# Loading the three bf16 terms of the layer-3 queries one by one, each after its own store

## The chip, the cores and the metric

The kernel runs on one core of one Trainium2 chip. The metric is the device time of one execution in microseconds (us); lower is better.

## The reference

Eight batches go through four cross-attention layers in a row. The change lies in the last one, layer 3. Cut to what matters, it computes for every batch (c = 128 channels, 16 heads of d = 8, 256 query and 256 key positions):

```
q = einsum('oc,bct->bot', Wq, x) + bq      # x: what layer 2 returned
k = einsum('oc,bct->bot', Wk, kv) + bk     # kv: the context
v = einsum('oc,bct->bot', Wv, kv) + bv
attn = softmax(einsum('bhqd,bhdk->bhqk', q * d ** -0.5, k))     # d = 8
mean = einsum('bhqk,bhkd->bhqd', attn, v)
ex2  = einsum('bhqk,bhkd->bhqd', attn, v * v)
std  = sqrt(relu(ex2 - mean * mean))
out  = (instance_norm(x) * std + mean) * mask
```

## The kernel before

The batches b = 0 to 7 follow each other, and within a batch the layers 1, 2 and 3; layer 0 of batch b + 1 is laid between them. Each engine has its program written out in order: SP issues the transfers (DMAs), PE the matmuls, ACT, DVE and POOL the rest, and semaphores join them. An engine whose next instruction waits does nothing else, so on SP every later transfer waits too.

**The terms.** A head of layer 3 has only 8 channels. To get fp32-like products from bf16 matmuls, queries and keys are each cut into three bf16 terms: `h` (the value rounded to bf16), `m` (what is left, rounded) and `l` (what is left of that). They are made in the tile `parts` (128 channels x 3 terms x 256 positions), whose rows are heads times channels. The matmul wants another layout: in `Qx` and `Kx` (partitions x 16 heads x 256 positions) the channels and terms of a head stand below each other on partitions 0 to 71, so that one product over 100 partitions sums all nine pairs of terms. Rows 72 to 99 hold the mask and the shift by the row maximum.

**The way of the terms.** One store per term goes from `parts` to a scratch tensor in DRAM, `q_parts` or `k_parts` (3 terms x 8 channels x 4096 values), and three loads bring 24 rows each back. Each load has 24 rows of 8 KB, 192 KB in all. For the nine pairs, one side repeats a term three times in a row (24 rows of one term) and the other lists the three terms (8 rows of each) three times. Before the change, `Kx` has the repeated order and `Qx` the listed one:

```
for j in range(3):      # in key_terms, L596
    sp.dma_start(Kx[24 * j:24 * j + 24], k_parts[j:j + 1].to_broadcast([3, 8, NH * D]))\
for j in range(3):      # in query_terms, L604
    sp.dma_start(Qx[24 * j:24 * j + 24], q_parts).then_inc(ld_qx, 16)
```

**Who makes the query terms.** ACT rounds `h` from the projection of `q3` (`highs3`, L1329). DVE takes the rest (L1747) and makes `m` and `l` (L1757, L1759) between other work, a few us later. ACT and POOL do the same for the keys earlier in the batch (L1501, L1973, L1975). SP stores a term when its semaphore stands (`store_terms`, L587).

**Who waits for them.** PE's `scores3(b, 0)` waits for all of `Kx` and `Qx` (`ld_kx`, `ld_qx`) before its first product, L883 in the profile. Before it PE has layer 0's scores of the next batch and the maxima of layer 3 (L700, L725, L731); these take their own bf16 copies of queries and keys, not `Qx`. After it come seven more such groups of `scores3`, between other units in an order written out in `BOTH` (`LAST3` for the last batch, which has no layer 0 beside it; there `idle_products`, L909, fill PE's time with products that nobody reads).

**What SP does around it.** In a batch: the layer-2 weights, the stores and loads of the key terms, the stores and loads of the query terms, the weights of layer 1 (`load_mlp`, `WA` and `WB`, 1024 KB each, L529 and L530), the inputs of the next batch (`load_inputs`, `load_z`), and the regrouping of layer 3's sums through `scratch`.

Of the kernel before, what the change touches and what calls it, by code (L numbers as in the profile page):

```python
# [30 lines left out]
D = 256  # L31
NH = 16
# [150 lines left out]
def build(nc, z_in, ctxT_in, ctx_in, mask1, mask2, mask3, w0, wo, w1qk, w1v, w1o, w1a, w1b,  # L183
          w2qkv, w2o, w2a, w2b, w3, cols_in, rows_in, ident_in, hmask_in, sel_in, out):
    with ExitStack() as stack:
        def sb(name, shape, dt=F32):
            return stack.enter_context(nc.sbuf_tensor(name, shape, dt))
# [4 lines left out]
        def sem(name):  # L192
            return stack.enter_context(nc.semaphore(name))
# [76 lines left out]
        Qx = sb("Qx", [P, NH, D], BF16)  # L270
        Kx = sb("Kx", [P, NH, D], BF16)
# [30 lines left out]
        q_parts, k_parts = (nc.dram_tensor(n, [3, 8, NH * D], BF16, kind="Internal").ap() for n in ("q_parts", "k_parts"))  # L302
# [17 lines left out]
        def col(name, i=0):  # L320
            return cols[:, COLS[name][0] + i:COLS[name][0] + i + 1]
# [4 lines left out]
        def row(name):  # L326
# [2 lines left out]

        ld_w0 = [sem(f"ld_w0_{i}") for i in range(4)]  # L330
        ld_w0v = sem("ld_w0v")
        st_k, st_q, ld_kx, ld_qx = sem("st_k"), sem("st_q"), sem("ld_kx"), sem("ld_qx")
        const_x = sem("const_x")
        (ld_proj, ld_cols, ld_par, ld_rows, ld_wo, ld_w1, ld_w2, ld_w3, ld_mlp, ld_ctx, ld_res, ld_msk, ld_c3,
         st_u3, st_out) = (sem(n) for n in (
# [16 lines left out]
        s_K3h, s_K3r, s_K3m, s_K3l, s_Q3h, s_Q3r, s_Q3m, s_Q3l = (  # L352
            sem("s_" + n) for n in ("K3h", "K3r", "K3m", "K3l", "Q3h", "Q3r", "Q3m", "Q3l"))
# [20 lines left out]
        def is_last(b):  # L374
            return isinstance(b, int) and b == B - 1
# [72 lines left out]
        def wait(eng, s, value):  # L448

            if isinstance(value, int) and value <= 0:  # L450
                return
            eng.wait_ge(s, value)
# [74 lines left out]
        def _(sp):  # L527
# [52 lines left out]
                sp.wait_ge(s_V0, 2 * n)  # L580
                sp.dma_start(W0[:, 4], w0[4 + n % 2]).then_inc(ld_w0v, 16)

            def store_terms(b, scr, ready, stored):

                for i, s in enumerate(ready):
                    sp.wait_ge(s, b + 1)
                    sp.dma_start(scr[i].rearrange("d (h l) -> h d l", l=D), parts[:, i, :]).then_inc(stored, 16)  # L587

            def key_terms(b):

                store_terms(b, k_parts, (s_K3h, s_K3m, s_K3l), st_k)
                sp.wait_ge(s_msk, N_MSK * b + 3)
                sp.dma_start(Kx[72:73], b3row[0:1, :].unsqueeze(1).to_broadcast([1, NH, D])).then_inc(ld_kx, 16)
                sp.wait_ge(st_k, 48 * b + 48)
                for j in range(3):
                    sp.dma_start(Kx[24 * j:24 * j + 24], k_parts[j:j + 1].to_broadcast([3, 8, NH * D]))\  # L596
                        .then_inc(ld_kx, 16)

            def query_terms(b):

                store_terms(b, q_parts, (s_Q3h, s_Q3m, s_Q3l), st_q)
                sp.wait_ge(st_q, 48 * b + 48)
                for j in range(3):
                    sp.dma_start(Qx[24 * j:24 * j + 24], q_parts).then_inc(ld_qx, 16)  # L604

            def body(b):

                if not is_last(b):
                    load_values(2 * b + 3)
                sp.wait_ge(s_x1, b + 1)  # L610
                load_mlp(w2a, w2b)
                if not is_first(b):
                    store_batch(b - 1)
                if b + 2 < B:
                    load_values(2 * b + 4)
                key_terms(b)
                query_terms(b)
                if not is_last(b):
                    load_mlp(w1a, w1b)
                    load_inputs(b + 1)  # L620
                    if b + 2 < B:
                        load_z(b + 2)

                for half in range(0 if is_last(b) else 2):
                    sp.wait_ge(s_U3, 2 * b + half + 1)
                    sp.dma_start(scratch[:, 2 * half:2 * half + 2], U3[:, 2 * half:2 * half + 2, :])\
                        .then_inc(st_u3, 16)
                    sp.wait_ge(st_u3, 32 * b + 16 * half + 16)
                    for q in range(3):
                        for g in (2 * half, 2 * half + 1):  # L630
                            src = scratch.rearrange("(s r) g i -> g s r i", r=32)[g][:, 8 * q:8 * q + 8, :]
                            sp.dma_start(C3[32 * g:32 * g + 32, q, :], src).then_inc(ld_c3, 16)
# [640 lines left out]
        def _(act):  # L1273
            def take(o, name):

                bank, n = o.at(name)
                act.wait_ge(gp_full[bank], n + 1)
                return GP[bank]
# [137 lines left out]
            def body(b):  # L1416
# [75 lines left out]
                def keys3(i):  # L1492
                    if i != 1:
                        return
                    g = take(o, "k3")
                    for e in range(2):
                        ins = act.activation(K3b[:, e, :], g[:, 0:D], ACT.Identity, scale=hmask[:, 8 + e:9 + e],
                                             bias=col("bkm", e))
                    ins.then_inc(s_K3b, 1)
                    wait(act, st_q, 48 * b)  # L1500
                    act.activation(parts[:, 0, :], g[:, 0:D], ACT.Identity, bias=col("bk")).then_inc(s_K3h, 1)  # L1501
                attention12(b, 2, 0.25, keys3)
                if more:
                    mixed(b, [2])
# [399 lines left out]
        def _(pool):  # L1904
# [65 lines left out]
            def keys3(b):  # L1970

                pool.wait_ge(s_K3r, b + 1)
                pool.tensor_copy(parts[:, 1, :], rest_k).then_inc(s_K3m, 1)  # L1973
                pool.wait_ge(s_K3m, b + 1)
                pool.tensor_tensor(parts[:, 2, :], rest_k, parts[:, 1, :], ALU.subtract).then_inc(s_K3l, 1)  # L1975

            def body(b):
# [27 lines left out]
                apart.wait((s_o3, b))  # L2005
                pool.tensor_scalar(m3[:], m3row[:], 0.0, None, ALU.add).then_inc(s_msk, 1)
                keys3(b)
                power(b, 3)
                pool.tensor_tensor(res2[:], xa[:], row("pb"), ALU.add).then_inc(s_res2, 1)
# [124 lines left out]
```

## Time and profile before

| | |
|---|---|
| median of 3 runs | 1008.47 us (1007.87 to 1010.12) |
| profiled execution, its own time | 1012.25 us |
| its span, first to last instruction | 1010.5 us |
| mean granted TensorE clock | 0.995 |
| busy: PE, DVE, ACT, POOL | 935.5, 559.5, 456.2, 292.4 us |
| share of the chain that ended last: PE, DMA | 67%, 5% |

The profile lists the busy time of every engine, the chain of work that ended last (followed back from the last instruction, at each step to what released it), and who waited for whom. A row of a timeline has start and duration in us, the engine (SPq is SP's queue of issues), the line, the operation, what it writes from what, how many instructions were merged, and in brackets the idle time of the engine before it with its releaser. DMA share is the mean busy share of the core's 16 DMA engines.

### The profile page before, as it was taken

What the parts mean: (1) busy time and instruction counts of PE and PEld (TensorE: products, weight loads), DVE (VectorE), ACT (ScalarE), POOL (GpSimd) and SP (SyncE); (2) the same over time, 40 slices, a digit from 0 to 9 for tenths busy, and PEclk for the clock granted to TensorE, in tenths of its full rate; (3) what the DMA queues carried; (4) which work ended last, traced back from release to release, by engine and by line L of the source; (5) the groups of instructions that cost most, each with busy time, mean ns of one, the idle gap of its engine ahead of it and who ended that gap; (6) DMA issues with size and microseconds to landing.
All of it is one profiled execution on the core that took longest, in us unless ns stands there. A gap on an engine that the chain in (4) does not pass through costs nothing.

```text
span 1010.5 us, 21161 instructions
## 1 busy us (share of the span) xinstructions
PE 935.5 (93%) x8450; PEld 596.5 (59%) x8450; DVE 559.5 (55%) x890; ACT 456.2 (45%) x795; POOL 292.4 (29%) x402
## 2 busy tenths in 40 slices
PE   6989989999999998999999999999999999898995
PEld 5555764666647665567646666466665675455552
DVE  4344467445664557555675456644576546664554
ACT  2423444445444544445544454345544454442424
POOL 5230222334212432115322242124321243222401
PEclk9999999999999999999999999999999999999999
DMA  9500324113140132303241130401414031310220
GB/s 362 190 38 2 125 75 146 38 43 136 36 156 19 57 139 81 108 6 126 79 146 38 43 134 32 154 28 43 141 50 143 14 120 44 119 53 2 98 55 6
DMA packets 36728, 86.54 MB, mean 86 GB/s; under 512 B 8472, under 2 KB 26008, under 8 KB 28824
## 3 DMA queue, kind: packets, MB, share of 16 engines
q1 hardware_dynamic: 36632, 85.18, 24.5%
q8 instruction: 69, 1.13, 0.5%
q14 instruction: 27, 0.22, 0.1%
HBM read 77.24 MB, written 7.86 MB: 84 GB/s over the span
## 4 chain that ended last, share of the span: by engine, by line
PE 67%; DVE 12%; issue 6%; DMA 5%; ACT 5%; SPq 4%; POOL 1%; DVEq 0%; ACTq 0%; POOLq 0%
PE GP L1107 6%; PE GP L1118 6%; PE GP L660 6%; DVE nm L1592 5%; PE GP L662 5%; PE PV L821 4%; PE GP L1091 4%; PE PV L860 3%; PE GP L900 3%; PE SC L883 3%; PE PV L1031 3%; DMA Qx<-q_parts 2%; PE GP L667 2%; PE SC L1018 2%; PE SC L804 2%
## 5 line engine op out<-in xcount | busy, mean ns | idle before, releaser
L1592 DVE TENSOR_REDUCE nm<-MX 128x4 bf16<-128x1024 f32 (+1 forms) x168 | 206.4, 1229 | 125.3 <-PE MX L751 48.3
L1363 ACT ACTIVATE Pr<-SC 128x1024 f32<-128x1024 f32 x120 | 122.7, 1023 | 153.6 <-PE SC L883 76.9
L1966 POOL TENSOR_TENSOR Psum<-Pr 128x512 f32<-128x512 f32 x64 | 81.5, 1274 | 163.4 <-ACT Pr L1363 163.4
L660 PE MATMUL GP<-zP,W 128*128 128x128 f32 x512 | 106.3, 290 | 7.7 <-DMA W<-w 7.7
L662 PE MATMUL GP<-uP,W 128*128 128x128 f32 x512 | 99.7, 277 | 0.0
L660 PEld LDWEIGHTS GP<-zP,W 128*128 128x128 f32 x512 | 78.3, 193 | 29.0 <-issue 27.3
L1392 ACT ACTIVATE Pr<-SC,bcol 128x512 f32<-128x512 f32 x96 | 60.8, 685 | 51.3 <-PE SC L1018 50.7
L1934 POOL TENSOR_TENSOR stat<-stat,half 128x1 f32<-128x1 f32 x24 | 13.7, 570 | 224.4 <-DVE stat L1800 171.2
L662 PEld LDWEIGHTS GP<-uP,W 128*128 128x128 f32 x512 | 78.5, 194 | 0.0
L821 PE MATMUL PV<-Pr,V 128*64 128x256 f32 x512 | 70.8, 398 | 0.0
L1118 PE MATMUL GP<-WB,work 128*128 128x256 f32 x256 | 60.8, 386 | 6.5 <-DVE work L1731 6.4
L804 PE MATMUL SC<-Q,K 64*128 64x256 f32 x512 | 65.8, 376 | 0.0
L1107 PE MATMUL GP<-oT,WA 128*128 128x128 f32 x512 | 61.2, 278 | 0.9 <-ACT oT L1428 0.5
L1107 PEld LDWEIGHTS GP<-oT,WA 128*128 128x128 f32 x512 | 58.4, 192 | 4.9 <-issue 2.9
L1118 PEld LDWEIGHTS GP<-WB,work 128*128 128x128 f32 x256 | 46.8, 190 | 18.3 <-issue 12.9
L1285 ACT ACTIVATE Q<-GP,cols 128x256 f32<-128x256 f32 x56 | 23.5, 471 | 71.5 <-PE GP L662 71.5
L1939 POOL TENSOR_TENSOR stat<-stat,half 128x2 f32<-128x2 f32 x8 | 5.7, 710 | 170.9 <-DVE stat L1657 170.9
L1719 DVE TENSOR_TENSOR work<-GP,cols 128x512 f32<-128x512 f32 x32 | 22.1, 692 | 57.6 <-PE GP L1107 57.6
L1018 PE MATMUL SC<-work,K 64*128 64x512 f32 x192 | 52.6, 617 | 0.0
L804 PEld LDWEIGHTS SC<-Q,K 64*128 64x128 f32 x512 | 49.5, 188 | 4.8
L1926 POOL TENSOR_TENSOR work<-xb,hmask 128x512 f32<-128x512 f32 x32 | 32.6, 1041 | 52.2 <-DVE Q12b L1709 52.0
L1293 ACT ACTIVATE V<-GP 128x512 f32<-128x512 f32 x32 | 19.1, 597 | 62.4 <-PE GP L668 62.4
(221 smaller groups left out, 1750.3 us busy)
## 6 DMA issues: line engine op xcount, KB each, us to landing
W<-w SPq DMA_DIRECT2D x20, 1024.0 KB, 5.3
WA<-w1a SPq DMA_DIRECT2D x8, 1024.0 KB, 7.2
WB<-w1b SPq DMA_DIRECT2D x8, 1024.0 KB, 9.5
WA<-w2a SPq DMA_DIRECT2D x8, 1024.0 KB, 4.8
WB<-w2b SPq DMA_DIRECT2D x8, 1024.0 KB, 7.0
Kx<-k_parts SPq DMA_DIRECT2D x24, 192.0 KB
Qx<-q_parts SPq DMA_DIRECT2D x24, 192.0 KB
scratch<-U SPq DMA_DIRECT2D x14, 256.0 KB, 2.0
```

The costliest lines, as they stand in the source:

```text
L660: pe.matmul(dst, W0[:, piece, 2 * s, at:at + P], zP[:, s * P:s * P + P], start=True, stop=False)
L662: mm = pe.matmul(dst, W0[:, piece, 2 * s + 1, at:at + P], uP[:, s * P:s * P + P], start=False, stop=True)
L804: mm = pe.matmul(SC[r][:, kc * D:kc * D + D], K0[half, k, kc * P:kc * P + P], Q0[half, k, :], start=False, stop=True, skip_group_check=True)
L821: mm = pe.matmul(bank[64 * j:64 * j + 64, i * D:i * D + D], V0[:, kc, h * 64:h * 64 + 64], Pr[:, (n + j) % 4, kc * D:kc * D + D], start=(k ...
L1018: pe.matmul(SC[r][:].rearrange("p (t l) -> p t l", l=P), K[half, c, kc * P:kc * P + P], Q12[half, 4 * c:4 * c + 4, :], start=False, stop=True,
L1091: mm = pe.matmul(g[:, m * width:m * width + width], W[:, c, m * P:m * P + P], rhs(c), start=(c == 0), stop=(c == 1), skip_group_check=True)
L1107: mm = pe.matmul(g[:, j * P:j * P + P], WA[:, c, f * P:f * P + P], oT[:, c, :], start=(c == 0), stop=(c == 1), skip_group_check=True)
L1118: mm = pe.matmul(g[:, 0:D], G[:, f * P:f * P + P], WB[:, f, :], start=(f == 0), stop=(f == 7))
L1363: act.activation(Pr[:, n % 4:n % 4 + 2, :], SCP[:], ACT.Exp, scale=8.0 ** -0.5 if L else 0.125)\
L1392: act.activation(Pr[:, n % 4, :], SC[n % 2][:], ACT.Exp, bias=bias, scale=scale)\
L1592: dve.tensor_reduce(dst, MXP[:].rearrange("p i (a k) -> p i a k", a=a), AX_X, ALU.max, negate=True)\
L1966: pool.tensor_tensor(Psum[:, c % 4, :].rearrange("p (a l) -> p a l", l=D), two[:, :, 0:D], two[:, :, D:2 * D], ALU.add)\
```

## The change

`Qx` and `Kx` exchange their orders. `Kx` now gets all three terms by each of its three loads, and `Qx` gets one term by each, repeated three times. So the load of a query term needs only that term's store, and each store gets a semaphore of its own (`st_q[0..2]`). In all batches but the last, SP issues the load of `h` between the store of `h` and that of `m`; in the last batch all three stores come first.

```
-                sp.wait_ge(st_k, 48 * b + 48)
...
+            def load_term(b, i):
+
+                sp.wait_ge(st_q[i], 16 * b + 16)
+                sp.dma_start(Qx[24 * i:24 * i + 24], q_parts[i:i + 1].to_broadcast([3, 8, NH * D])).then_inc(ld_qx, 16)
...
                 for j in range(3):
-                    sp.dma_start(Kx[24 * j:24 * j + 24], k_parts[j:j + 1].to_broadcast([3, 8, NH * D]))\
-                        .then_inc(ld_kx, 16)
+                    sp.dma_start(Kx[24 * j:24 * j + 24], k_parts).then_inc(ld_kx, 16)
 
             def query_terms(b):
 
-                store_terms(b, q_parts, (s_Q3h, s_Q3m, s_Q3l), st_q)
-                sp.wait_ge(st_q, 48 * b + 48)
-                for j in range(3):
-                    sp.dma_start(Qx[24 * j:24 * j + 24], q_parts).then_inc(ld_qx, 16)
+                store_terms(b, q_parts, ((0, s_Q3h, st_q[0]),))
+                if not is_last(b):
+                    load_term(b, 0)
+                store_terms(b, q_parts, ((1, s_Q3m, st_q[1]), (2, s_Q3l, st_q[2])))
+                for i in range(3 if is_last(b) else 2):
+                    load_term(b, i if is_last(b) else i + 1)
...
-                    wait(act, st_q, 48 * b)
+                    wait(act, st_q[0], 16 * b)
...
             def keys3(b):
 
                 pool.wait_ge(s_K3r, b + 1)
+                for stored in st_q[1:]:
+                    wait(pool, stored, 16 * b)
                 pool.tensor_copy(parts[:, 1, :], rest_k).then_inc(s_K3m, 1)
```

The last two edits guard `parts`, which the key terms of a batch overwrite: ACT waits only for the store of `h` of the batch before, and POOL for the stores of `m` and `l`.

SP's order in batch 0 before, from the stores of the key terms on (a row is line, transfer, shape of the destination as issued, and the semaphores waited for; `st_k` and `st_q` count landed stores):

```order
L587 DMA k_parts<-parts 16x8x256 [waits s_K3l]
L593 DMA Kx<-b3row 1x16x256 [waits s_msk]
L596 DMA Kx<-k_parts 24x1x4096 [waits st_k]
L596 DMA Kx<-k_parts 24x1x4096 x2
L587 DMA q_parts<-parts 16x8x256 [waits s_Q3h]
L587 DMA q_parts<-parts 16x8x256 [waits s_Q3m]
L587 DMA q_parts<-parts 16x8x256 [waits s_Q3l]
L604 DMA Qx<-q_parts 24x4096 [waits st_q]
L604 DMA Qx<-q_parts 24x4096 x2
L529 DMA WA<-w1a 128x2048
```

The same place in the changed kernel:

```order
L593 DMA k_parts<-parts 16x8x256 [waits s_K3l]
L599 DMA Kx<-b3row 1x16x256 [waits s_msk]
L602 DMA Kx<-k_parts 24x4096 [waits st_k]
L602 DMA Kx<-k_parts 24x4096 x2
L593 DMA q_parts<-parts 16x8x256 [waits s_Q3h]
L587 DMA Qx<-q_parts 24x1x4096 [waits st_q0]
L593 DMA q_parts<-parts 16x8x256 [waits s_Q3m]
L593 DMA q_parts<-parts 16x8x256 [waits s_Q3l]
L587 DMA Qx<-q_parts 24x1x4096 [waits st_q1]
L587 DMA Qx<-q_parts 24x1x4096 [waits st_q2]
L530 DMA WA<-w1a 128x2048
```

One `Qx` load has moved ahead of two stores, and the shapes 24x1x4096 and 24x4096 have changed sides. PE, ACT, DVE and POOL keep their instructions in their order.

## Rows read from the trace of the kernel before

**Rows 1.** The page, part 4: share of the chain by engine.
```profile
PE 67%; DVE 12%; issue 6%; DMA 5%; ACT 5%; SPq 4%; POOL 1%; DVEq 0%; ACTq 0%; POOLq 0%
```

**Rows 2.** What ended the idle time ahead of L883: us in all, times.
```profile
  DMA Qx<-q_parts: 6.0, 5
```

**Rows 3.** Timeline of PE: the first L883 products of batches 0, 1, 2, 4, 6, 7.
```profile
166.08 0.60 PE L883 MATMUL SC<-Qx,Kx 100*128 100x256 bf16 x4 [0.30 <-DMA Qx<-q_parts]
...
284.26 0.61 PE L883 MATMUL SC<-Qx,Kx 100*128 100x256 bf16 x4
...
403.18 0.60 PE L883 MATMUL SC<-Qx,Kx 100*128 100x256 bf16 x4 [0.72 <-DMA Qx<-q_parts]
...
641.19 0.60 PE L883 MATMUL SC<-Qx,Kx 100*128 100x256 bf16 x4 [1.64 <-DMA Qx<-q_parts]
...
880.58 0.60 PE L883 MATMUL SC<-Qx,Kx 100*128 100x256 bf16 x4 [1.79 <-DMA Qx<-q_parts]
...
986.51 0.60 PE L883 MATMUL SC<-Qx,Kx 100*128 100x256 bf16 x4 [1.57 <-DMA Qx<-q_parts]
```

**Rows 4.** Timeline of SP: the stores of the query terms, batches 0, 1, 2, 4, 6, 7.
```profile
152.33 5.88 SPq L587 DMA_DIRECT2D q_parts<-parts  x3
...
270.89 5.88 SPq L587 DMA_DIRECT2D q_parts<-parts  x3
...
389.01 5.88 SPq L587 DMA_DIRECT2D q_parts<-parts  x3
...
626.11 5.88 SPq L587 DMA_DIRECT2D q_parts<-parts  x3
...
865.34 5.88 SPq L587 DMA_DIRECT2D q_parts<-parts  x3
...
977.00 2.13 SPq L587 DMA_DIRECT2D q_parts<-parts  x3
```

**Rows 5.** Timeline of SP, batch 1: key loads, stores of m and l, query loads.
```profile
254.38 2.30 SPq L596 DMA_DIRECT2D Kx<-k_parts  x3
...
275.56 1.21 SPq L587 DMA_DIRECT2D q_parts<-parts  x2
...
278.24 1.15 SPq L604 DMA_DIRECT2D Qx<-q_parts  x3
```

**Rows 6.** Stretches of batch 1 after the key loads; last columns: clock, DMA share, GB/s.
```profile
259.00:261.50 2.50, 2.50 (x24) 2.50 (x24) 0.94 (x2) 0.30 (x1) 0.00 (x0) 1.00 0.19 79
261.50:264.00 2.50, 2.50 (x29) 1.67 (x27) 1.64 (x3) 1.34 (x3) 0.00 (x0) 1.00 0.19 79
264.00:265.00 1.00, 0.20 (x4) 0.00 (x0) 0.95 (x2) 0.84 (x3) 0.00 (x0) 1.00 0.00 0
```

**Rows 7.** Transfers that touch q_parts: time from issue to landing.
```profile
DMA to landing us min/median/max: 2.0/2.0/3.7
```

**Rows 8.** The chain that ended last, batch 6.
```profile
875.04 5.30 DMA Qx<-q_parts
```

**Rows 9.** Stretches of batch 1: query loads beside the weights, then the weights alone.
```profile
282.00:284.00 2.00, 2.00 (x24) 0.83 (x22) 1.40 (x2) 0.27 (x1) 1.27 (x1) 1.00 0.99 274
...
285.00:286.00 1.00, 1.00 (x10) 0.43 (x9) 0.72 (x1) 0.99 (x1) 0.00 (x0) 1.00 1.00 418
```

**Rows 10.** Stretches of batches 4 and 6 after L883; the column after POOL is the clock.
```profile
643.00:644.00 1.00, 1.00 (x8) 0.29 (x6) 0.00 (x0) 0.00 (x0) 0.00 (x0) 0.50 1.03 434
883.00:884.00 1.00, 1.00 (x10) 0.30 (x8) 0.00 (x0) 0.00 (x0) 0.00 (x0) 0.50 0.99 379
```

**Rows 11.** Timeline of PE: the fourth L883 group of batches 1 and 4.
```profile
291.51 0.61 PE L883 MATMUL SC<-Qx,Kx 100*128 100x256 bf16 x4
...
649.62 0.61 PE L883 MATMUL SC<-Qx,Kx 100*128 100x256 bf16 x4
```

**Rows 12.** Timeline, batch 0: the input load issued last, and its first reader.
```profile
168.10 0.36 SPq L575 DMA_DIRECT2D zP<-z_in  x1
...
184.68 0.49 PE L660 MATMUL GP<-zP,W 128*128 128x128 f32 x2
```

More of the change, by code:

```diff
@@ L331, in build @@
         ld_w0v = sem("ld_w0v")
-        st_k, st_q, ld_kx, ld_qx = sem("st_k"), sem("st_q"), sem("ld_kx"), sem("ld_qx")
+        st_k, ld_kx, ld_qx = sem("st_k"), sem("ld_kx"), sem("ld_qx")
+        st_q = [sem(f"st_q{i}") for i in range(3)]
         const_x = sem("const_x")
@@ L581, in load_values, with store_terms @@
                 sp.dma_start(W0[:, 4], w0[4 + n % 2]).then_inc(ld_w0v, 16)
-            def store_terms(b, scr, ready, stored):
-                for i, s in enumerate(ready):
+            def load_term(b, i):
+                sp.wait_ge(st_q[i], 16 * b + 16)
+                sp.dma_start(Qx[24 * i:24 * i + 24], q_parts[i:i + 1].to_broadcast([3, 8, NH * D])).then_inc(ld_qx, 16)
+            def store_terms(b, scr, terms):
+                for i, s, stored in terms:
                     sp.wait_ge(s, b + 1)
@@ L589, in key_terms @@
             def key_terms(b):
-                store_terms(b, k_parts, (s_K3h, s_K3m, s_K3l), st_k)
+                store_terms(b, k_parts, ((0, s_K3h, st_k), (1, s_K3m, st_k), (2, s_K3l, st_k)))
                 sp.wait_ge(s_msk, N_MSK * b + 3)
```

## The prediction

> **What bounds the kernel now.** I read the chain that ended last first: PE holds 67% of it, DMA only 5% [rows 1]. So a transfer matters only where PE stands still for it. The second view is that of L883, the first product that reads `Qx`: its engine sat idle 6.0 us in all for `Qx<-q_parts`, at 5 of its starts [rows 2]. The timeline places four of the waits and shows a batch without one: 0.30 us in batch 0, none in 1, 0.72 in 2, 1.64 in 4, 1.79 in 6, 1.57 in 7 [rows 3]; batches 3 and 5 look like batch 1. So 6.0 us is all that faster query loads can give back directly, and a later landing costs in every batch, since batch 1 has hardly any slack.
>
> The third view is SP's timeline. Call T the start of the store of `h`. L883 starts at T + 13.75, 13.37, 14.17, 15.08 and 15.24 us in batches 0, 1, 2, 4, 6 [rows 3, 4]. Whatever lies above 13.37 is a wait, and it isn't given back later: T of batch 1 to T of batch 2 is 118.12 us, T of 0 to T of 1 is 118.56, so 0.44 longer for an L883 that was 0.38 late. From batch 4 to 6 it is 239.23; with 118.12 for batch 5, batch 4 has 121.11, which is 2.99 more for an L883 that was 1.71 late and a slow TensorE clock behind it (below) [rows 4]. I count each us of delay in full.
>
> **What the change does to the loads.** The two kinds of load carry the same 192 KB, but not alike. The order puts the shape 24x1x4096, today the keys', on the queries. What it costs is in the trace: SP takes 2.30 us to issue three of these, against 1.15 for three of the shape 24x4096 [rows 5]. And while the key loads run, the DMA engines are 0.19 busy and move 79 GB/s, for 5 us on end [rows 6]: 3 of 16 engines (0.1875), and one load after the other. 196.6 KB at 79 GB/s are 2.49 us for each. The three were issued from 254.38 and the first stretch without traffic is 264 to 265; with 264.5 as their end they took 10.12 us, so one alone takes 10.12 - 2 x 2.49 = 5.15 us to land, and each further one 2.49. The query loads in today's shape took 5.30 us from the issue of the third to the landing of all three [rows 8], beside other traffic.
>
> The Trainium skill (DMA: Bandwidth & Descriptors, Rules for kernel authors) speaks against the change here: a leading broadcast of c copies confines a DMA to at most c engines, and the trace agrees, with 0.19 for c = 3. With that page's ~27 GiB/s per engine a load would need an estimated 2.26 us instead of 2.49, 0.69 less for three loads, which over eight batches would lower the sum below by 5.5 us.
>
> **Step by step, batches 0 to 6.** The store of `h` lands at T + 2.0 [rows 7]; its load is issued then and lands at T + 2.05 + 5.15 = T + 7.2. SP is done issuing at T + 2.8, and the store of `m` is issued at T + 4.67 (275.56 - 270.89) [rows 4, 5], so SP's new wait delays nothing queued behind it. But the stores run over all engines, three of which still hold the load of `h` until T + 7.2. I let the stores of `m` and `l` finish 0.35 us after it (unknown; 0 would be unhindered passing behind it). Then the load of `m` is issued at T + 7.55, lands at T + 12.7, the load of `l` behind it at T + 15.19, and L883 follows 0.24 later, as in batch 6 (875.04 + 5.30 to 880.58) [rows 3, 8]: T + 15.43. Against the present offsets that is 1.68 in batch 0, 2.06 in each of 1, 3 and 5, 1.26 in 2, 0.35 in 4, 0.19 in 6: **9.7 us**.
>
> By the Trainium skill (DMA: Bandwidth & Descriptors, Queues, rings and completion order) one engine consumes the descriptors of a queue in ring order, which is this holding up; no row of before has a small store right behind such a load. What it would be without it stands among the rivals.
>
> **Batch 7.** All three loads come after the issue of the third store, at 977.00 + 2.13 = 979.13 [rows 4]. They take the keys' 10.12 us, and L883 starts at 989.49 instead of 986.51: **3.0 us**.
>
> **The weights behind.** `WA` and `WB` are issued right after the load of `l`. Today's query loads beside them make the DMA move 274 GB/s where the weights alone make 418 [rows 9], a factor of 1.5. If the load of `l` is slowed so, it costs 1.25 us a batch, 8.7 in seven; if three engines keep their 26 GB/s each (79 / 3, and 418 / 16 is the same), nothing. I take 0.3 a batch, nearer to the latter, as few engines write: **2.1 us**.
>
> **The clock.** In the waits of batches 4 and 6 PE stood 1.64 and 1.79 us, and behind them the granted clock was 0.50 (1.2 of 2.4 GHz) [rows 3, 10]. From the first to the fourth L883 group takes 8.43 us in batch 4, 7.25 in batch 1 [rows 3, 11]: 1.18 us for one such fall. Behind the 0.72 and the 1.57 it didn't fall. With L883 2.1 us and more behind its place in each batch, and 4.5 in the last, I expect falls in three of batches 0, 1, 2, 3, 5 and in the last: 4 x 1.18 = **4.7 us** (bounds: none, and all six, 7.1).
>
> **At no cost.** The key loads get faster; they had landed by 264.5 and are read at 284.26 [rows 3, 6], so 19.8 us of PE's other work hide them either way. Were that gone, they would gain what the queries lose. The guards of ACT and POOL wait for stores that landed some 90 us earlier. The loads behind the queries are issued about 0.6 us later, and on three engines stand behind the load of `l`; the last is read 16.6 us after its issue [rows 12]. Only beyond that would it cost, us for us. PE, ACT, DVE and POOL run the same instructions.
>
> **Sum.** 9.7 + 3.0 + 2.1 + 4.7 = 19.5 us. The terms are differences within the profiled execution (span 1010.5, its own time 1012.25, so 1.75 around the span, and 3.8 above the median); on the median of 1008.47 they give **1028 us**, and the profiled execution should read about 1032. A measurement of this kernel tells 0.2%, 2 us, from no change.
>
> **Rivals.**
> - *Stores not held up* (0.10). If `m` and `l` pass the load of `h`, the load of `m` is issued at T + 4.67 + 2.0 and L883 is at T + 14.6: +0.8, 3 x 1.2, +0.4, -0.5, -0.7, with batch 7 at +3.0: +6.7. Its waits of some 1.2 us are shorter than the 1.57 behind which the clock held, so two falls go and one (batch 7) comes: -1.2. With some contention 1015 us.
> - *The loads run side by side* (0.04), faster. If the loads of different terms got different engines, the last would land 5.15 us after the landing of `l`'s store, hardly any wait would be left, and the two clock falls would go: up to -6.0 - 2.4, about 1002 us. It decides if the DMA share goes well above 0.19 with only these loads in flight. The key loads, issued 0.77 us apart, speak against it: 0.19 throughout [rows 5, 6].
> - *Hidden anyway* (0.02). PE would have to find its delay again in later idle; the T to T times above say that it doesn't. 1008 us.
> - *Worse than the sum* (0.04). The weights slow the load of `l` by the full 1.25 us and the clock falls everywhere: 12.7 + 8.7 + 7.1 = 28.5, 1037 us and beyond.
>
> My forecast has the remaining 0.80, by itself 1021 (12.7 us alone) to 1037. The range reaches down to the first rival: 1015 to 1037. Faster 0.04, same 0.02, slower 0.94.
>
> **What would show it.** SP's three `Qx` issues take 0.77 us each and the keys' three 1.15 together. A DMA share of 0.19 between T + 4 and T + 7. L883 waits for `Qx` in all eight batches, some 2 us or more each, 16 to 24 us in all, at T + 15.4 to 15.7. The stores of `m` land after T + 7. T to T is 120.2 us or more in every batch, 121.4 where the clock fell. Wrong would be: an L883 before T + 15, a share above 0.19 for these loads alone, or T to T times that don't follow L883's lateness.

## The result: 5% slower, and the profile after

| | before | after |
|---|---|---|
| median of 4 runs each, on one chip | 1008.9 us (1007.87 to 1010.12) | 1059.1 us (1058.07 to 1062.91) |
| ratio, 95% interval | | 1.0504 [1.0475, 1.0533] |
| profiled execution: own time, span | 1012.25, 1010.5 us | 1058.65, 1056.9 us |
| mean granted TensorE clock | 0.995 | 0.976 |

The direction was right, and the size was not: 50 us on the medians and 46.4 on the spans, against 19.5 forecast and a range that ended at 1037. (The profiled execution of before is 3.4 us slower than the median of its kernel, the one of after is not; hence the two figures.) L883 of before is L890 now. The page of the changed kernel: the shares of the chain that ended last (for [rows 1]), and the issues of the layer-1 weights (count, KB each; median us from issue to landing).

```profile
PE 64%; DVE 11%; DMA 10%; issue 6%; ACT 4%; SPq 3%; POOL 1%; DVEq 0%; ACTq 0%; POOLq 0%
...
WA<-w1a SPq DMA_DIRECT2D x8, 1024.0 KB, 10.4
WB<-w1b SPq DMA_DIRECT2D x8, 1024.0 KB, 13.6
```

The same two issues on the page of before:

```profile
WA<-w1a SPq DMA_DIRECT2D x8, 1024.0 KB, 7.2
WB<-w1b SPq DMA_DIRECT2D x8, 1024.0 KB, 9.5
```

DMA's share of the chain doubled, from 5% to 10%. And two transfers that the change doesn't touch are late: `WA` and `WB` landed 7.2 and 9.5 us after their issue before, now 10.4 and 13.6.

What released L890, in the view of its line (us, times):

```profile
  DMA Qx<-q_parts: 40.3, 8
```

The idle time before the first score product went from 6.0 us [rows 2] to 40.3. PE waits in all 8 batches, 3.75 to 5.65 us each, where before it waited in 5, at most 1.79 us. Four of its starts on PE's timeline (batches 0, 1, 6, 7; in brackets the idle time before), for [rows 3]:

```profile
171.15 0.59 PE L890 MATMUL SC<-Qx,Kx 100*128 100x256 bf16 x2 [5.65 <-DMA Qx<-q_parts]
...
296.69 1.01 PE L890 MATMUL SC<-Qx,Kx 100*128 100x256 bf16 x4 [5.40 <-DMA Qx<-q_parts]
...
922.48 0.60 PE L890 MATMUL SC<-Qx,Kx 100*128 100x256 bf16 x4 [3.75 <-DMA Qx<-q_parts]
...
1031.65 0.58 PE L890 MATMUL SC<-Qx,Kx 100*128 100x256 bf16 x2 [4.94 <-DMA Qx<-q_parts]
```

SP's timeline in batch 1 and the stores and loads of batch 7, for [rows 4, 5]:

```profile
261.02 1.15 SPq L602 DMA_DIRECT2D Kx<-k_parts  x3
...
277.84 0.54 SPq L593 DMA_DIRECT2D q_parts<-parts  x1
279.86 0.82 SPq L587 DMA_DIRECT2D Qx<-q_parts  x1
282.51 1.20 SPq L593 DMA_DIRECT2D q_parts<-parts  x2
285.41 1.51 SPq L587 DMA_DIRECT2D Qx<-q_parts  x2
286.96 0.43 SPq L530 DMA_DIRECT2D WA<-w1a  x1
...
1018.78 2.31 SPq L593 DMA_DIRECT2D q_parts<-parts  x3
1021.16 2.30 SPq L587 DMA_DIRECT2D Qx<-q_parts  x3
```

T is 277.84 in batch 1. The load of `h` goes out at T + 2.02, the load of `m` at T + 7.57 (forecast 7.55), that of `l` 0.78 behind it, and `WA` at T + 9.12. Up to here everything is as predicted. The first product was to start at T + 15.43 and starts at T + 18.85. The piece of the chain in batch 1 names what is between (start, us, what):

```profile
282.51 2.89 DMA q_parts<-parts
285.40 0.02 issue
285.41 0.74 SPq L587
286.15 0.04 issue
286.19 10.25 DMA Qx<-q_parts
296.44 0.25 issue
296.69 1.01 PE SC L890 x4
```

The two loads issued from 285.41 had landed 11.03 us later; 7.64 were forecast. The stretches of the same batch and one of batch 7 (us; busy of PE, PEld, DVE, ACT, POOL with counts; granted clock; DMA share; GB/s), for [rows 6, 9, 10]:

```profile
281.00:283.00 2.00, 2.00 (x22) 1.07 (x20) 1.91 (x4) 1.44 (x3) 0.00 (x0) 1.00 0.17 61
290.00:292.00 2.00, 1.29 (x16) 0.40 (x14) 1.09 (x2) 0.00 (x0) 0.57 (x1) 1.00 1.09 250
292.00:294.00 2.00, 0.00 (x0) 0.00 (x0) 0.67 (x1) 0.00 (x0) 0.00 (x0) 1.00 0.94 205
294.00:296.00 2.00, 0.00 (x0) 0.00 (x0) 0.00 (x0) 0.00 (x0) 0.00 (x0) 0.88 1.04 229
296.00:298.00 2.00, 1.31 (x6) 0.73 (x8) 0.00 (x0) 0.22 (x1) 0.00 (x0) 0.50 0.98 345
1026.50:1029.00 2.50, 0.20 (x1) 0.00 (x0) 0.52 (x1) 0.00 (x0) 0.00 (x0) 1.00 0.19 79
```

Three things are to be seen. With a query load alone in flight the share is 0.17 to 0.19 (three engines of 16 are 0.1875), as forecast. With the weights beside it all 16 engines count as busy (0.94 to 1.09), yet move 205 to 250 GB/s, where the weights alone moved 418 [rows 9]; the rate goes up as soon as the query loads have landed at 296.44. And PE, which stands from 291.3 to 296.7, comes back at half clock.

### The profile page after: what moved, and what is told of

Same layout as the page of the kernel before. It is cut to its first block, busy times and chain, and to the rows that moved or that the text cites. A ratio compares the mean times of both kernels' runs of the same rounds, so it can differ in the third digit from the quotient of the medians.

```text
span 1056.9 us, 21168 instructions
## 1 busy us (share of the span) xinstructions
PE 950.4 (90%) x8450; PEld 601.2 (57%) x8450; DVE 558.6 (53%) x890; ACT 455.8 (43%) x795; POOL 291.4 (28%) x402
## 4 chain that ended last, share of the span: by engine, by line
PE 64%; DVE 11%; DMA 10%; issue 6%; ACT 4%; SPq 3%; POOL 1%; DVEq 0%; ACTq 0%; POOLq 0%
DMA Qx<-q_parts 7%; PE GP L1114 6%; PE GP L1125 6%; PE GP L667 6%; PE GP L669 4%; DVE nm L1599 4%; PE PV L828 4%; PE SC L890 3%; PE GP L1098 3%; PE PV L867 3%; PE GP L907 3%; PE PV L1038 3%; DMA q_parts<-parts 2%; PE GP L674 2%; PE SC L1025 2%
## 5 line engine op out<-in xcount | busy, mean ns | idle before, releaser
L890 PE MATMUL SC<-Qx,Kx 100*128 100x256 bf16 x256 | 43.6, 297 | 41.6 <-DMA Qx<-q_parts 40.3
L1941 POOL TENSOR_TENSOR stat<-stat,half 128x1 f32<-128x1 f32 x24 | 13.6, 568 | 224.4 <-DVE stat L1807 171.2
L828 PE MATMUL PV<-Pr,V 128*64 128x256 f32 x512 | 75.1, 417 | 0.0
L890 PEld LDWEIGHTS SC<-Qx,Kx 100*128 100x128 bf16 x256 | 23.1, 104 | 61.2 <-issue 54.2
## 6 DMA issues: line engine op xcount, KB each, us to landing
WA<-w1a SPq DMA_DIRECT2D x8, 1024.0 KB, 10.4
WB<-w1b SPq DMA_DIRECT2D x8, 1024.0 KB, 13.6
```

What stands on the lines that cost most here:

```text
L828: mm = pe.matmul(bank[64 * j:64 * j + 64, i * D:i * D + D], V0[:, kc, h * 64:h * 64 + 64], Pr[:, (n + j) % 4, kc * D:kc * D + D], start=(k ...
L890: mm = pe.matmul(SC[j][:, e * D:e * D + D], Kx[0:100, h, kc * P:kc * P + P], Qx[0:100, h, :], start=True, stop=True, skip_group_check=True)
```

## The experiments

The offsets below are from T to the first product of `scores3`. Their sum over batches 0 to 6 is 98.37 us before and 129.51 after. A ratio is the time of a kernel over that of the kernel before on the same chip, with its 95% interval.

**1. The weights issued behind the query loads.** Theory: the traffic beside the loads of `m` and `l` takes the missing 3 us a batch. Rival: the loads themselves are slower than those of the keys. The edit adds one wait to the changed kernel, and holds back everything that SP issues behind it:

```diff
+                    sp.wait_ge(ld_qx, 48 * b + 48)
                     load_mlp(w1a, w1b)
```

> The changed kernel, with one wait more: SP issues the layer-1 weights WA and WB only after all query loads have landed. Theory (the weights behind halve the pace of the last two query loads): the first product that reads Qx starts at T + 15.4 instead of T + 18.2 to 19.1 (T: issue of the store of h), so 7 x 3.1 = 21 us less plus shorter spells of slow clock, in all about 1030 us. Rival (loads that read what was just stored are slow by themselves, whatever runs beside them): it stays at T + 18 to 19 and the time at 1059 us.

Measured: 1026.84 us, ratio 1.0178 [1.0152, 1.0204], clock 0.992. L891 (the same product) waits half as long as in the changed kernel:

```profile
  DMA Qx<-q_parts: 19.6, 8
```

SP and PE in batch 1 of this kernel:

```profile
272.86 0.54 SPq L593 DMA_DIRECT2D q_parts<-parts  x1
...
280.60 1.51 SPq L587 DMA_DIRECT2D Qx<-q_parts  x2
288.28 0.36 SPq L530 DMA_DIRECT2D WA<-w1a  x1
...
288.51 0.60 PE L891 MATMUL SC<-Qx,Kx 100*128 100x256 bf16 x4 [2.20 <-DMA Qx<-q_parts]
```

The page of this kernel on the weights:

```profile
WA<-w1a SPq DMA_DIRECT2D x8, 1024.0 KB, 4.8
WB<-w1b SPq DMA_DIRECT2D x8, 1024.0 KB, 7.0
```

T is 272.86 and the product starts at T + 15.65; over the batches 0 to 6 the offsets are 14.94 to 16.72, sum 108.77 (forecast 15.43 each, 108.01). From issue to landing the pair takes 7.68 us (280.60 to 288.28), forecast 7.64. The weights land in 4.8 and 7.0 us instead of 10.4 and 13.6. So the query loads and the weights are each late beside the other, and the traffic beside the loads is worth 32 us of the 50, the clock that it costs included. Not all of the weights' lateness need be a slower pace: in the changed kernel `WA` lands some 1.2 us after the query loads (these land 9.2 us after its issue, the median of batches 0 to 6, read from the start of the product that waited for them), so it may in part only stand behind them. The added wait is not a remedy for the change: the kernel stays 1.8% slower than before.

**2. All three loads behind all three stores.** It tells what the early load of `h` is worth in the changed kernel's shape.

```diff
-                store_terms(b, q_parts, ((0, s_Q3h, st_q[0]),))
-                if not is_last(b):
-                    load_term(b, 0)
-                store_terms(b, q_parts, ((1, s_Q3m, st_q[1]), (2, s_Q3l, st_q[2])))
-                for i in range(3 if is_last(b) else 2):
-                    load_term(b, i if is_last(b) else i + 1)
+                store_terms(b, q_parts, ((0, s_Q3h, st_q[0]), (1, s_Q3m, st_q[1]), (2, s_Q3l, st_q[2])))
+                for i in range(3):
+                    sp.wait_ge(st_q[i], 16 * b + 16)
+                for i in range(3):
+                    load_term(b, i)
```

> The changed kernel, with its load of h no longer early: all three query loads are issued after all three stores have landed, in the three-engine shape. Theory (three engines serve the loads one after the other, 2.49 us each, and the early load of h hides one of them): the loads are issued from T + 7.35 and one more 2.5 us stands on the path in batches 0 to 6, L890 at T + 21 to 22 and about 1077 us. Rival (the early load gains nothing, as it holds up the stores of m and l by as much): 1059 us.

Measured: 1091.13 us, ratio 1.0820 [1.0795, 1.0845], clock 0.962, offsets 21.4 to 24.0 us. The wait of the first product in this kernel:

```profile
  DMA Qx<-q_parts: 71.3, 8
```

The direction is as expected, the size larger (1077 expected): the early load is worth 32 us. All three loads now lie beside the weights, so 192 KB more go at the slow pace; that this makes the difference to the 18 us expected is argued, no run takes it apart. So the change holds a gain, the load of its own store, and a loss, the shape, and the loss is the larger.

**3. The same loads on eight engines.** If the three engines are the trouble, the same bytes should be fast when the outer dimension is 8. By the Trainium skill (DMA: Bandwidth & Descriptors, Why a DMA increments its semaphore by 16 and not by 1), a DMA goes to the largest number of engines up to 16 that divides both outer dimensions: 3 for 3x8 into 24 rows, 12 for 24 rows of one list into 24, 8 for 8x3. The traces agree for the first two, with 0.19 above (3/16 is 0.1875) and 0.76 in experiment 4 (12/16 is 0.75). This edit changes the order of the channels within a term, for the queries and the keys alike:

```diff
-                sp.dma_start(Qx[24 * i:24 * i + 24], q_parts[i:i + 1].to_broadcast([3, 8, NH * D])).then_inc(ld_qx, 16)
+                sp.dma_start(Qx[24 * i:24 * i + 24], q_parts[i].unsqueeze(1).to_broadcast([8, 3, NH * D])).then_inc(ld_qx, 16)
...
-                    sp.dma_start(Kx[24 * j:24 * j + 24], k_parts).then_inc(ld_kx, 16)
+                    sp.dma_start(Kx[24 * j:24 * j + 24], k_parts.rearrange("i d n -> d i n")).then_inc(ld_kx, 16)
```

> The changed kernel, with the rows of a term in another order: the 24 rows are channel by channel, each repeated three times, so that the source has 8 outermost rows instead of 3 (Kx's loads read the terms in the same order). Each term still goes alone and as early. Theory (the cost is the width of the load, not the splitting by terms): a DMA share near 0.5 and 200 GB/s for one load, the store of m no longer held up, the last load landed by T + 12 to 13, no wait of PE for Qx in batches 0 to 6 and a shorter one in 7: 1000 to 1004 us. Rival (separate loads and the wait in SP's order cost as such): no better than 1009 us.

Measured: 1005.42 us, ratio 0.9969 [0.9958, 0.9980]: 0.3% faster than before, and just short of the 1000 to 1004 us expected. The first product's wait, and SP in batch 1:

```profile
  DMA Qx<-q_parts: 2.2, 2
```

```profile
271.45 0.58 SPq L593 DMA_DIRECT2D q_parts<-parts  x1
...
276.12 1.23 SPq L593 DMA_DIRECT2D q_parts<-parts  x2
278.14 1.44 SPq L587 DMA_DIRECT2D Qx<-q_parts  x2
```

The load of `m` goes out at T + 6.69 here, 2.02 after its store; in the changed kernel it was at T + 7.57. The same store, issued at the same T + 4.67, thus lands 0.9 us sooner with the wider load of `h` in front of it, in four of seven batches; in the other three the load of `m` goes out at T + 7.23 to 7.93. That bears out the holding up of the stores, though not in every batch. The offsets are 13.38 to 13.51 in all batches but the first (14.60), and no half-clock stretch is left but the one at the very end.

**4. The kernel before with the same wait as in 1.** The forecast read from [rows 9] that the weights slow today's query loads by 1.5. Then before should gain from it too.

```diff
+                    sp.wait_ge(ld_qx, 48 * b + 48)
                     load_mlp(w1a, w1b)
```

> The kernel before, with the layer-1 weights issued only after all query loads have landed. Theory (the weights also slow the query loads of the kernel before): its waits for Qx of 0.3 to 1.8 us in batches 0, 2, 4, 6 shrink or go, with them the slow clock behind batches 4 and 6, and the time falls by 4 to 7 us, to 1002 to 1005. Rival (contention only arises beside three-engine loads): 1009 us.

Measured: 1007.38 us, ratio 0.9995 [0.9984, 1.0006]: no difference, where 1002 to 1005 us were expected. SP's issues in batch 1 of this kernel, and two stretches while the query loads alone are in flight:

```profile
277.89 1.14 SPq L604 DMA_DIRECT2D Qx<-q_parts  x3
283.35 0.36 SPq L529 DMA_DIRECT2D WA<-w1a  x1
```

```profile
279.00:282.00 3.00, 2.75 (x28) 1.64 (x28) 2.25 (x3) 1.85 (x3) 1.27 (x1) 1.00 0.76 167
...
281.00:282.00 1.00, 0.75 (x8) 0.45 (x10) 0.80 (x2) 0.93 (x1) 0.00 (x0) 1.00 0.74 139
```

With nothing beside them the loads of before move 167 GB/s in the mean of 3 us, 139 in the last of these (221 in the first), at a share of 0.74 to 0.76. So 12 engines run these loads slowly by themselves, and the 274 GB/s of [rows 9] are no measure of a slowing by the weights. From the issue of the first load the three take 5.0 to 5.7 us here, and 5.3 to 6.1 beside the weights in the batches of before that wait for them; so the weights cost them tenths of a us. (The waits of the first product add up to 4.1 us here and to 6.0 before, each in one execution; the medians show no gain.) The expectation missed, and with it goes the forecast's only row on contention.

**5. Eight engines, all loads last.** Experiment 3 with the order of experiment 2.

> The eight-engine kernel (24 rows of a term channel by channel, source with 8 outermost rows), with all three query loads issued only after all three stores have landed, as in the kernel before. Theory (the early start is worth something only where PE waits): loads issued from T + 7.35 (later in even batches) with 0.77 us of issue each end at T + 13.4 to 14.5; a wait of some 0.3 to 1 us a batch, batch 7 about 0.8 us later, in all 4 to 8 us above the eight-engine kernel, 1009 to 1013. Rival (the early start gains nothing, the width is all): 1005.

Measured: 1033.29 us, ratio 1.0209 [1.0188, 1.0231], clock 0.987, offsets 14.9 to 18.5 us. The wait of the first product:

```profile
  DMA Qx<-q_parts: 21.8, 8
```

So in the eight-engine shape too, loading each term behind its own store is worth 2.4% (1.0209 against 0.9969); I had expected 4 to 8 us. The width counts as well: in the same order the 12-engine loads of before are 2.1% faster than these. Eight-engine loads issued late are slowed by the weights too: from the issue of the first to the first product 7.3 to 9.1 us pass in batches 0 to 6, and 6.4 in batch 7, which has no weights behind. A stretch of batch 1:

```profile
286.00:288.00 2.00, 1.73 (x20) 0.54 (x16) 1.09 (x2) 0.00 (x0) 1.01 (x1) 1.00 0.99 246
```

**6. Eight engines and the weights behind.** Experiments 3 and 1 together.

> The eight-engine kernel, with the layer-1 weights issued only after all query loads have landed. Theory (contention with the weights is small once the loads are short): the last load lands at T + 11 to 12.5 in place of 12.3 to 14.4, the remaining wait of 1.2 us in batch 0 goes, 1003.5 to 1005. Rival (its remaining waits come from stores that land late, not from the weights): no change, 1005.4.

Measured: 1004.6 us, ratio 0.9932 [0.9917, 0.9947], the lowest of all. The wait of the first product, and SP and PE in batch 1:

```profile
  DMA Qx<-q_parts: 0.8, 1
```

```profile
270.05 0.58 SPq L593 DMA_DIRECT2D q_parts<-parts  x1
...
276.88 1.44 SPq L587 DMA_DIRECT2D Qx<-q_parts  x2
281.88 0.34 SPq L530 DMA_DIRECT2D WA<-w1a  x1
...
283.43 0.61 PE L891 MATMUL SC<-Qx,Kx 100*128 100x256 bf16 x4
```

The first product starts at T + 13.38 in all of batches 0 to 6, and in batch 1 the weights, which wait for the landing, go out 1.55 us before that product. One wait is left, in batch 7. In one stretch with only the query loads in flight the share is 0.54 with 197 GB/s, half of the 16 engines at 25 GB/s each (197 / 8):

```profile
279.00:280.00 1.00, 1.00 (x14) 0.80 (x10) 0.63 (x1) 0.34 (x1) 1.00 (x1) 1.00 0.54 197
```

The step from experiment 3 to this one wasn't timed on one chip: the ratios, each against before on its own chip, lie apart, and the waits went from 2.2 to 0.8 us.

**7 to 10 and 12. What do the loads and the weights share?** Each of these is the changed kernel with one thing about the three-engine loads altered, as a single profiled run. The candidates were the DRAM rows that are read three times over (7, 9), and the partitions that are written (8, 10, 12). In all of them layer 3's scores are computed from other, misplaced or missing terms, so they serve for timing alone. In 12, `h` and `m` go into `Qx` one after the other and `l` into `Kx`, for which SP gets two more waits; these make batch 7 later (15.32 against 12.87 us) and hardly touch the others. The lines that differ, cut to the source or the target:

```diff
# 7: read another tensor, 8 KB rows of it
+src = ident_in.rearrange("(a r) c -> a (r c)", a=8).unsqueeze(0).to_broadcast([3, 8, 2048])
# 9: 24 rows that all differ
+src = sel_in.rearrange("(a r) h k -> a (r h k)", r=2)[0:63].rearrange("(j r) n -> j r n", j=3)[:, 4 * i:4 * i + 8]
# 8: m and l into partitions 104 to 127
+dst = (Qx[0:24], Kx[104:128], Qx[104:128])[i]
# 10: every third partition
+sp.dma_start(Qx[i:72:3], q_parts[i:i + 1].to_broadcast([3, 8, NH * D]))
# 12: all three into partitions 0 to 23
+dst = Kx[0:24] if i == 2 else Qx[0:24]
```

> The changed kernel, whose three query loads, in the same shape on three engines and at the same moments, read 8 rows of 8 KB of an input tensor (the identity matrix) in place of the stored terms; layer 3's scores are computed from these, so that its output isn't layer 3's. Theory A (the slow pace of the loads beside the weights comes from reading the small scratch tensor): the loads run at full pace, first product that reads Qx at T + 15.4, 1030 us. Theory B (it comes from where or how they write): unchanged, T + 18 to 19, 1059 us. Theory C (any three-engine load of a row read three times beside a 16-engine stream does it): unchanged too; the next kernel then parts B from C.

> The changed kernel, whose loads of m and l write 24 rows on partitions 104 to 127 in place of 24 to 71 (the term of h stays where it was); m and l are thus left out of the scores. Theory B (the loads and the weights write the same partitions at the same time): with the rows moved away from the partitions that the weights' first engines write, the pace changes, the first product at T + 15.4 to 17, and 1030 to 1045 us. Theories A and C (source, or total): T + 18 to 19, 1059 us.

> The changed kernel, whose query loads, still in three groups of 8 rows on three engines, read 24 different rows of an input tensor (spread over half a megabyte) in place of 8 rows three times; layer 3's scores are computed from these, so that its output isn't layer 3's. Theory C (three engines reading the same row at the same time beside the weights halve the pace): full pace, first product that reads Qx at T + 15.4, 1030 us. Theory D (any load on three engines with the weights behind it does, whatever it reads): T + 18 to 19, 1059 us.

> The changed kernel, whose query loads write every third partition of 0 to 71 in place of 24 adjacent ones; the rows of the terms no longer stand where Kx has their partners, so layer 3's scores aren't the reference's. Theory F (writes into a few adjacent partitions beside the weights' writes cause the slow pace): first product at T + 15.4 to 17, 1030 to 1045 us. Theories C and D: T + 18 to 19, 1059 us.

> [...] Rival (a load on three engines ahead of the weights does it wherever it writes): T + 18 to 19, 1059 us. [...]

| | time, us | offsets of batches 0 to 6, their sum | `WA`, `WB` land after |
|---|---|---|---|
| changed kernel | 1059.1 | 17.2 to 19.1, 129.51 | 10.4, 13.6 |
| 7 other source | 1063.91 | 18.2 to 20.9, 133.65 | 10.3, 13.8 |
| 9 distinct rows | 1068.64 | 19.2 to 20.9, 138.50 | 10.5, 14.1 |
| 8 other partitions | 1054.39 | 16.9 to 18.6, 126.78 | 10.1, 13.2 |
| 10 every third partition | 1059.94 | 17.1 to 19.1, 126.46 | 9.3, 13.1 |
| 12 partitions 0 to 23 | 1060.9 | 18.1 to 19.4, 129.32 | 9.1, 13.0 |

If one of these were the cause, its sum would come down toward the 108.77 of experiment 1. None comes down by more than 3.1 of the 20.7 us, and two go up. (Compare the sums and not the times: in 10 the first T came 4.3 us late. Of the 9.0 us more in 9, 4.6 lie ahead of the load of `m`, whose store lands later there.) It is not the repeated reading of one row, nor which tensor is read, nor any of these three placements. Which partitions an engine writes for the weights no trace shows, so whether engines that write near each other get in each other's way stays untested.

**11 and 13. The same bytes, not written into SBUF.** The loads of `m` and `l` go to a scratch tensor in DRAM, in 11 in one piece per engine (64 KB), in 13 in rows of 8 KB set apart, so that each piece is as large as in the changed kernel.

```diff
+q_copy = nc.dram_tensor("q_copy", [3, 24, NH * D], BF16, kind="Internal").ap()                      # 11
+q_copy = nc.dram_tensor("q_copy", [3, 24, NH * D + 256], BF16, kind="Internal").ap()[:, :, 0:NH * D]  # 13
+dst = q_copy[i] if i else Qx[0:24]
```

> The changed kernel, whose loads of m and l, still from the stored terms on three engines, write a scratch tensor in DRAM in place of Qx; m and l are left out of the scores. Theory W (the halved pace beside the weights comes from the writes into SBUF): the weights run at full pace behind them, landing some 5 to 8 us after their issue in place of 10 and 14, and the first product comes at T + 15.4 to 16, 1030 us. Theory R (it comes from the engines or the reading side): unchanged, T + 18 to 19, 1059 us.

> As the kernel whose loads of m and l write a scratch tensor in DRAM (m and l are left out of the scores), with the rows of that tensor 512 bytes apart, so that each transfer is again 24 rows of 8 KB as it is into Qx. Theory W (the halved pace beside the weights comes from writing into SBUF): T + 15 to 15.5 as with whole blocks, 1027 us. Rival (the whole blocks of 64 KB were what made that kernel fast): T + 18 to 19, 1059 us.

Measured: 1026.92 us with offsets of 15.0 to 16.7 (sum 108.81) in 11, and 1035.24 with 14.7 to 16.9 (sum 111.40) in 13. Expected were 1030 and 1027; 13 lies between its theory and its rival, much nearer to the theory. With the weights not behind them, in batch 7 of 13, these loads show a share of 0.17 to 0.23 and 74 to 98 GB/s, so they too run on three engines. A stretch of 13 in which the loads of `m` and `l` and the weights are all in flight, in batch 1 (the weights issued at 283.69, the query loads landed by 290.8):

```profile
287.00:290.00 3.00, 0.62 (x10) 0.23 (x6) 1.23 (x1) 0.00 (x0) 0.00 (x0) 1.00 1.00 393
```

With the same loads into SBUF it was 205 to 250 GB/s. The weights' landings, from the pages of 11 and of 13:

```profile
WA<-w1a SPq DMA_DIRECT2D x8, 1024.0 KB, 7.4
WB<-w1b SPq DMA_DIRECT2D x8, 1024.0 KB, 11.1
```

```profile
WA<-w1a SPq DMA_DIRECT2D x8, 1024.0 KB, 7.3
WB<-w1b SPq DMA_DIRECT2D x8, 1024.0 KB, 11.4
```

Of the 20.7 us that the offsets of the changed kernel lie above those of experiment 1 (129.51 - 108.77), 18.1 are gone when the same rows go to DRAM (129.51 - 111.40), and 2.6 stay; with 64 KB pieces nothing stays. The weights still land later than alone (7.3 against 4.8 us), though 393 GB/s move in all: in 13 `WA` lands some 1.0 us after the query loads, as it does in the changed kernel (1.2), and that part fits a standing behind them on the three engines, which no run shows by itself. So most of the slowing of the query loads needs their writes into SBUF beside those of the weights. What part of that way it is, these runs don't tell; none of the placements tried made a difference.

## Why the prediction was right in direction and wrong in size

The terms of the sum against what the traces give. The parts add up to the difference of the spans, 46.4.

| term | forecast | measured | from |
|---|---|---|---|
| batches 0 to 6, offsets without the weights | 9.7 | 10.4 | 108.77 - 98.37, experiment 1 |
| batch 7 | 3.0 | 3.4 | 12.87 - 9.51 |
| the weights behind | 2.1 (0 to 8.7) | 20.7 | 129.51 - 108.77 |
| the clock | 4.7 (0 to 7.1) | 11.9 | the rest of 46.4 |

- **What bounds the kernel, and no give-back: right.** T to T is 125.81 us in batch 1 against 118.12, and L890 5.48 later there. All of the delay came through, and 2.2 us more by the clock. The rival "hidden anyway" falls.
- **The shape's cost: right.** SP needs 0.74 to 0.82 us for an issue and 1.15 for the keys' three, the share is 0.19 with 79 GB/s where such a load is alone, batch 7 lost 3.4 us for 3.0, and experiment 1 gives offsets within 0.5 us of 15.43 but for one batch (16.72), in which the store of `h` landed late (its load went out at T + 3.09). The rival "side by side" falls.
- **Stores held up: right, with luck in the size.** The load of `m` goes out at T + 7.09 to 7.80 in the changed kernel (7.55 forecast, of which 0.35 was a guess); free stores would have meant T + 6.67, and experiment 3 shows T + 6.70 in four batches. The rival of free stores falls.
- **The weights behind: the step that failed.** I bounded its cost by 1.25 us a batch, from a factor of 1.5 on the load of `l` alone, and took 0.3. It is 2.96 (20.7 / 7). Two errors are in it. The factor came from a stretch in which loads on 12 engines were slow by themselves (experiment 4), so it was no bound for loads on three. And only the load of `l` was counted as lying beside the weights, whereas the load of `m` is in flight too: it is issued 1.55 us before `WA`. Alone the pair takes 7.68 us, beside the weights 11.03. In its place the runs show that two loads on three engines into SBUF lose 3 us a batch beside the weights, and next to nothing of it when their target is in DRAM (experiments 1, 11, 13); why writes into SBUF do this stays open. The lower end, three engines that keep their 26 GB/s, was nearer to what I took and is refuted.
- **The clock: the second term that was mis-sized, and above its bound.** I had expected four falls of 1.18 us, from a wait of 1.64. The half-clock stretches are in all eight batches, and six of them last 6.8 us in place of 3.4. What T to T has grown beyond the delay of L890 is 1.95 to 2.46 us in a batch with a long one and 1.2 to 1.5 with a short one; these add to 13.6 in batches 0 to 6 (2.6 before), and with 1.25 in batch 7, less 0.3 for a first T that came earlier, they make the 11.9. A wait of 5 us is not priced by a row on a wait of 1.7. Most of this excess is the contention's: in experiment 1, with waits of 1.5 to 3.3 us in batches 0 to 6, only batches 1 and 4 fell behind a wait, and 7.
- **The landing and the end.** The loads behind the queries cost nothing to be seen. The key loads are faster and off the path, as said. (The text speaks of four waits that the timeline places; it lists five, and they are what [rows 3] has.)

The chance for "worse than the sum" was 0.04; that case had the right mechanism, with its price for the weights capped by the same wrong factor.

## What to carry to other kernels

Before a transfer is reshaped, count its engines by the outer dimension and read the DMA share of such a load in the trace; then ask what is issued right behind it, since here a load on three engines into SBUF with one on all 16 behind it made both late, and by far more than its bytes (3.4 us for the pair of query loads and 5.6 for `WA`, where the pair's 393 KB are 0.9 us at 418 GB/s). The gain of loading each piece behind its own store was real: 2 to 3% against the same shape with all loads last. Against the kernel before it came out only when the broadcast was put second (8x3 in place of 3x8), and was then 0.3%, since in the same order the eight-engine loads are slower than those of before (experiment 5). A price for waits and clock falls holds for waits of the length at which it was read, and for no longer ones.

## What the hardware did that I had not expected

- Loads into SBUF on 3 engines beside weights on 16 moved 205 to 250 GB/s in all at a share of 0.94 to 1.09; the weights alone move 418. The pair of query loads took 11.03 us in place of 7.68, and `WA` 10.4 in place of 4.8. The rows read (experiments 7, 9) and the partitions written (8, 10, 12) changed the sum of the seven offsets by -3.1 to +9.0 us of 20.7, and with a target in DRAM (11, 13) the query loads lost 0 to 0.4 us a batch in place of 2.96, while 393 GB/s moved in all. The cause within the way into SBUF stays open.
- A load of 24 rows on 12 engines with nothing beside it moves 167 GB/s in the mean of 3 us and 139 at its end, at a share of 0.74 to 0.76: 12 to 14 GB/s for an engine, where three engines reach 26 each and eight 25. Busy engines are no measure of bytes moved.
- The granted clock stayed at 0.50 (1.2 of 2.4 GHz) for 6.8 us behind waits of 5 us in most batches, and for 3.4 us behind 3.75 us in batch 6 and behind 5.16 in batch 3; so the length of the wait alone doesn't fix it.
